# Deformable convolution block on one core: four instead of five pairs gathered ahead, and the first chunk's expansion among the last tap products

## What is computed

```python
# layer 0
out = relu(bn(conv1x1(x, w1)))                  # 1024 -> 256 channels
offset = conv3x3(out, w_off, b_off)             # 18 channels: (dy, dx) of 9 taps
out = relu(bn(deform_conv3x3(out, offset, w2))) # 4 bilinear corners of 9 taps per pixel
x1 = relu(bn(conv1x1(out, w3)) + x)             # 256 -> 1024 channels
# layer 1
t, p, g = Wt @ x1, Wp @ x1, Wg @ x1             # 1024 -> 512 each
att = sum over pixels and channels of (1, p, p**2) * g
y = polynomial of second order in t with att
z = Wz @ y                                      # 512 -> 1024
return groupnorm(z) * gn_w + gn_b + x1
```

## Time and profile before

| | us |
|---|---|
| median of 3 runs (2628.82 to 2649.33) | 2645.32 |
| the profiled execution | 2640.11 |
| its span, first to last instruction | 2638.3 |
| TensorE, VectorE, ScalarE, POOL busy | 2333.8, 1561.7, 1233.0, 687.2 |

### The profile page before, as it was taken

How to read it: one execution, slowest core, us unless ns; L and a number is a source line. 1 busy time by engine, 2 the same in 40 slices (tenths; PEclk the granted TensorE clock), 3 DMA queues, 4 the chain that set the end, 5 groups by cost and what they waited for, 6 DMA issues and landing times.

```text
span 2638.3 us, 29349 instructions
## 1 busy us (share of the span) xinstructions
PE 2333.8 (88%) x10316; PEld 1921.2 (73%) x10316; DVE 1561.7 (59%) x3126; ACT 1233.0 (47%) x2393; POOL 687.2 (26%) x613
## 2 busy tenths in 40 slices
PE   7999997998863699999999999999999999987730
PEld 5888886777753587888888888888888878866530
DVE  4113115446345788889888889988842244544464
ACT  5444343333222455656655565665532244444454
POOL 0000013323341344455554455555400000000000
PEclk9999998898886899999999999999999999998875
DMA  7999999999996698899899889998931111144469
GB/s 255 285 290 269 293 277 336 311 350 294 341 286 254 234 327 316 320 342 340 316 327 328 314 325 339 340 321 326 324 134 68 56 36 48 64 147 160 157 245 390
DMA packets 328012, 691.68 MB, mean 262 GB/s; under 512 B 20664, under 2 KB 170040, under 8 KB 321464
## 3 DMA queue, kind: packets, MB, share of 16 engines
q1 hardware_dynamic: 225464, 327.28, 39.1%
q0 software_dynamic: 83968, 303.80, 32.4%
q10 hardware_dynamic: 18432, 58.73, 5.6%
HBM read 443.38 MB, written 246.35 MB: 261 GB/s over the span
## 4 chain that ended last, share of the span: by engine, by line
PE 73%; DMA 14%; DVE 6%; ACT 3%; SPq 2%; issue 2%; POOL 0%; ACTq 0%; DVEq 0%
PE bank L136 20%; PE bank L138 20%; PE bank L137 20%; DMA vwide<-vb 7%; PE bank L1239 4%; PE bank L1240 4%; PE bank L1241 4%; DMA xt<-x 2%; DVE z L1183 1%; PE bank L1263 1%; DMA tb<-t 1%; DMA xin<-in_x 1%; DVE zst L1153 1%; SPq L360 1%; DMA stage<-in_wl 1%
## 5 line engine op out<-in xcount | busy, mean ns | idle before, releaser
L555 POOL DMA_INDIRECT g<-vwide,tbl x576 | 667.3, 1158 | 853.6 <-DVE a L864 402.3
L136 PE MATMUL bank<-x1h,wlh 128*128 128x512 f32 x1536 | 603.8, 393 | 2.9 <-DVE x1l L1070 2.9
L138 PE MATMUL bank<-x1h,wll 128*128 128x512 f32 x1536 | 600.9, 391 | 0.0
L137 PE MATMUL bank<-x1l,wlh 128*128 128x512 f32 x1536 | 600.3, 391 | 0.0
L880 DVE SCALAR_TENSOR_TENSOR a<-g,tbl,a 128x256 f32<-128x256 f32 x1258 | 538.3, 476 | 28.6 <-DMA g<-vwide,tbl 27.0
L574 ACT ACTIVATE g<-g,tbl 128x256 f32<-128x256 f32 x972 | 409.9, 499 | 185.2 <-DMA g<-vwide,tbl 168.9
L136 PEld LDWEIGHTS bank<-x1h,wlh 128*128 128x128 f32 x1536 | 289.3, 188 | 64.1 <-issue 3.3
L138 PEld LDWEIGHTS bank<-x1h,wll 128*128 128x128 f32 x1536 | 289.0, 188 | 62.2
L137 PEld LDWEIGHTS bank<-x1l,wlh 128*128 128x128 f32 x1536 | 289.4, 188 | 61.0
L1239 PE MATMUL bank<-w2h,o1h 128*128 128x512 f32 (+1 forms) x640 | 249.0, 389 | 68.3 <-ACT vb L627 68.3
L627 ACT ACTIVATE vb<-bank 128x512 f32<-128x512 f32 (+1 forms) x320 | 166.9, 556 | 293.8 <-DMA vwide<-vb 212.4
(11 more groups left out here) (141 smaller groups left out, 3108.3 us busy)
## 6 DMA issues: line engine op xcount, KB each, us to landing
vwide<-vb SPq DMA_DIRECT2D x128, 1152.0 KB
xin<-in_x SPq DMA_DIRECT2D x64, 512.0 KB
xf<-in_x SPq DMA_DIRECT2D x32, 1024.0 KB
x<-xf ACTq DMA_DIRECT2D x32, 1024.0 KB, 6.6
out<-z SPq DMA_DIRECT2D x128, 256.0 KB, 4.4
xb<-x SPq DMA_DIRECT2D x38, 512.0 KB, 4.0
t<-ts ACTq DMA_DIRECT2D x64, 256.0 KB
tb<-t SPq DMA_DIRECT2D x16, 1024.0 KB, 5.1
```

The source lines that it names most:

```text
L136: nc.tensor.matmul(out, wh, xh, start=first, stop=False)
L137: nc.tensor.matmul(out, wh, xl, start=False, stop=False)
L138: return nc.tensor.matmul(out, wl, xh, start=False, stop=last)
L555: pool.indirect_dma_start(slot[:].rearrange("p a c -> p (a c)"), None, d["vwide"][img], bass.IndirectOffsetOnAxis(ap=at[:, i, tap(u), 0:1] ...
```

## The change

1. `ALONE` is 4, and `f_points` puts 36 units (four pairs) in the front: from step 10 on at points 1, 2, 3 and 5 of each step. All other units move up in P, still 18 per chunk. `sums_due` stores a pair's sum one point behind its completion instead of two, from the end of the front on.
2. Chunk 0's transposes, `o2(0)`, expansion, residual and x1 stand in steps 16 and 17, with buffers of their own: `ACL0` (in stage buffer 2), `O2H0`, `O2L0`, and PSUM banks 0 and 1. `x1_high(0, k)` stays behind the front. Pairs 0 and 1 are loaded in step 15, `XF` before the last four tiles' stores, and weight blocks 2 to 6 between those stores.
3. First step: three more x blocks ahead of W2; W2 is loaded and split in five column groups, behind `o1(0)`; the stores of zero pads go from SP's queue to POOL's.

```diff
-ALONE = 5
+ALONE = 4
...
-            if s == 9 and point > 2 or 10 <= s <= 16 and point not in (0, 4) or s == 17 and point < 6:
+            if s == 9 and point > 2 or s > 9 and point in (1, 2, 3, 5):
...
-... if e + 2 == k]
+... if e + (2 if e < len(F_ENDS) - 2 else 1) == k]
...
+    ACL0 = m.put("acl0", [128, TILES, CMID], at=STAGE_AT[2])
+    O2H0, O2L0 = (m.put(n, [128, KMID, NPX], f32r, at=R5 + at * KB) for n, at in (("o2h0", 5), ("o2l0", 20)))
...
@@ SP, first step
-            for k in range(KMID):
-                sp.dma_start(W2R[:, k, :], d["w2"][:, k, :]).then_inc(w2_in[k], 16)
+            for i in range(XR, 2 * XR):
+                load_x(i)
+            for j, (lo, hi) in enumerate(VGROUPS):
+                if j == 2:
+                    load_x(2 * XR)
+                sp.dma_start(W2R[:, :, lo:hi], d["w2"][:, :, lo:hi]).then_inc(w2_in[j], 16)
...
@@ SP, steps
                 if s == ALLC - 1:
-                    for w in range(3):
+                    for p in range(2):
+                        sp.wait_ge(ao_out, 16 * (p + 1))
+                        sp.dma_start(ACL0[:, 2 * p:2 * p + 2, :], d["acc"][p]).then_inc(acl0_in[p], 16)
+                    for w in range(2):
                         stage(w)
                 if s == ALLC:
-                    stage(3)
+                    for h in range(2):
+                        load_xf(0, h)
                 if s:
                     for t in range(TILES):
                         store_v(s - 1, t)
...
-                        if s == ALLC and t < 3:
-                            stage(4 + t)
+                        if s == ALLC and t == 0:
+                            sp.wait_ge(tr_done, TILES)
+                            stage(2)
+                        if s == ALLC and t:
+                            stage(2 + t)
+                        if s == ALLC and t == 3:
+                            stage(6)
...
             def load_acl(p):
-                if p == 0:
+                if p == 2:
                     for b in range(2):
                         sp.wait_ge(vb_out[b], vb_count(TILES * ALLC, b))
                 sp.wait_ge(ao_out, 16 * (p + 1))
-                at_least(sp, tr_done, 2 * p)
+                sp.wait_ge(tr_done, 2 * p)
                 sp.dma_start(ACL[:], d["acc"][p]).then_inc(acl_in, 16)
-            for h in range(2):
-                load_xf(0, h)
-            load_acl(0)
-            for w in range(7, 9):
-                stage(w)
-            load_acl(1)
-            for w in range(9, 12):
+            for w in range(7, 12):
                 stage(w)
...
@@ POOL: pads() moved here from SP
+            pool.wait_ge(o1_done, KMID * 3)
+            pads()
...
@@ ScalarE
                 if s == ALLC:
-                    for w in range(4):
+                    for w in range(2):
                         split_high(w)
...
                 if tiles:
                     v_evict(s - 1, 0)
+                if s == ALLC:
+                    o2(0)
+                if s == 0:
+                    w2_high(0)
+                    w2_high(1)
                 if 4 * s + XR + 3 < 4 * ALLC:
                     x_high(4 * s + XR + 3)
+                if s == 0:
+                    for j in range(2, len(VGROUPS)):
+                        w2_high(j)
...
+                if s == ALLC:
+                    for w in range(2, 4):
+                        split_high(w)
                 store_sums(7 * s + 3)
                 store_sums(7 * s + 4)
                 if tiles:
                     v_evict(s - 1, 2)
+                if s >= ALLC:
+                    x1_pair(0, 2 * (s - ALLC))
                 store_sums(7 * s + 5)
                 if tiles:
                     v_evict(s - 1, 3)
+                if s >= ALLC:
+                    x1_pair(0, 2 * (s - ALLC) + 1)
...
@@ VectorE: o2_low(0) behind f_gather(s, 1), residual_pair(0, ..) behind f_gather(s, 4) and (s, 6), s = 16 and 17
@@ TensorE
                 if 1 <= s <= ALLC:
                     taps(s - 1, 0)
+                if s == ALLC:
+                    for i in range(TILES):
+                        transposes(0, i)
+                if 1 <= s <= ALLC:
                     taps(s - 1, 1)
                 if s >= 2:
                     offsets(s - 2)
+                if s >= ALLC:
+                    expand_pair(0, 2 * (s - ALLC))
                 if 1 <= s <= ALLC:
                     taps(s - 1, 2)
                 if s >= 2:
                     select(s - 2)
+                if s >= ALLC:
+                    expand_pair(0, 2 * (s - ALLC) + 1)
                 if 1 <= s <= ALLC:
                     taps(s - 1, 3)
-            for i in range(TILES):
-                transposes(0, i)
-            for o in range(KIN):
-                expand(0, o)
```

More of the change, by code:

```diff
@@ L1043, in _ @@
                     nc.vector.tensor_copy(Y[2][:, :, 0:SIDE - 1], Y[1][:, :, 1:SIDE]).then_inc(ys_done, 1)
+                if s == ALLC:
+                    for w in range(2, 4):
+                        split_low(w)
                 f_gather(s, 4)
+                if s >= ALLC:
+                    residual_pair(0, 2 * (s - ALLC))
                 if s >= 2:
@@ L1105, in _ @@
             v.wait_ge(sums_set, IMGS)
-            o2_low(0)
-            for k in range(KIN):
-                residual(0, k)
             for k in range(KIN):
@@ L1227, in taps @@
                 tile, r = TILES * s + t, s % 3
-                if tile == 0:
-                    pe.wait_ge(w2l_done, KMID)
                 if t == 0:
@@ L1265, in select, with transposes, expand_pair @@
                 last.then_inc(op_done, 1)
+            def transposes(n, i):
+                if n == 0 and i == 0:
+                    pe.wait_ge(cst_in, 48)
+                    pe.wait_ge(o1_done, KMID * ALLC)
+                if n == 1 and i == 0:
+                    pe.wait_ge(off_done, ALLC)
+                if i == 0:
+                    at_least(pe, xr_done, KIN * n)
+                if i % 2 == 0 and n:
+                    pe.wait_ge(acl_in, 16 * (2 * n + i // 2 - 1))
+                elif i % 2 == 0:
+                    pe.wait_ge(acl0_in[i // 2], 16)
+                for k in range(KMID):
+                    tile = ACL[:, i % 2, 128 * k:128 * k + 128] if n else ACL0[:, i, 128 * k:128 * k + 128]
+                    last = nc.tensor.transpose(transpose_bank(n, k)[:, 128 * i:128 * i + 128], tile, IDENT[:])
+                last.then_inc(tr_done, 1)
+            def expand_pair(n, i):
+                high, low = o2_tiles(n)
+                if n == 0 and i == 0:
+                    pe.wait_ge(wl_done, 2)
+                if i == 0:
+                    pe.wait_ge(o2l_done, KMID * (n + 1))
+                if n == CHUNKS + 1 and i == 0:
+                    pe.wait_ge(coef_done, 1)
+                for o in (2 * i, 2 * i + 1):
+                    at_least(pe, xr_done, KIN * n + o - 3 if n else o - 1)
+                    for k in range(KMID):
+                        last = product(nc, expansion_bank(n, o)[:], W3H[:, k, 128 * o:128 * o + 128], W3L[:, k, 128 * o:128 * o + 128],
+                                       high[:, k, :], low[:, k, :], k == 0, k == KMID - 1)
+                    last.then_inc(w3_done, 1)
             for s in range(ALLC + 2):
```

219 lines of the change are left out of this document (108 added, 111 removed).

## The result

| | before | after |
|---|---|---|
| median of 4 runs, us | 2644.07 (2628.82 to 2649.33) | 2673.07 (2671.01 to 2678.99) |
| the profiled execution | 2640.11 | 2678.99 |
| its span | 2638.3 | 2677.0 |
| P's first project matmul, in the trace | 852.6 | 814.8 |
| Z begins | 2112.6 | 2150.7 |

The ratio of the times is 1.0131, with an interval of 1.0103 to 1.016. The kernel became slower by 1.3%; the forecast was 2666, +21 us, and the medians differ by 29. The two traces differ by 38.7: the profiled execution of the changed kernel is the slowest of its four, 6 us above the median, and that of the kernel before lies 4 us under its own.

The account below looks back on a forecast made before the run. P (twelve projections for each of 16 chunks) was taken as bound by TensorE, the late front by DMA. The front's -54 us and P's +75 gave +21: 2645 + 21 = 2666 us, range 2596 to 2712.

Parts of the forecast that it names:

- P: thirteen waits and the clock: In P, chunks 1 to 13 each lose 5.8 us to a TensorE stall and slower clock: +75 us.
- the front: Before P: fewer gathers, earlier first step, interleaved end; P starts at 798.4 instead of 852.57, -54 us, bounds -40 and -72.
- The wait: In P behind group 2, TensorE's transposes wait 4.2 us for the sums' store and load, 5.84 us each.
- Rival 1: In P, store and load together stay under 7.5 us, so only the front's gain is left: 2591; chance 0.15.
- rival 2: In P, stalls of 5 to 6 us and 3 us of half clock in 13 chunks: 2712; chance 0.17.
- The clock: In P, TensorE's matmuls run at half clock behind each stall: 1.6 us more per stall, bounds 0 and 3.2.
- One point instead of two gains nothing: In P, storing the sums one point behind the fold gains nothing: ScalarE already issued at 1048.16.
- There DMA is the bound: Late front's steps with gathers: DMA sets their time, 2.5 us per unit; nine units less give -22 us, bounds 21 and 27.
- What must still come last is the sixth weight block (w = 5): End of the front: this block, issued behind the last store and split before x1_high, adds 3 us before P.
- First step, -4: Start of the front: TensorE's first wait goes, the second shrinks by half; -4 us, bounds 0 and -10.
- The first chunk of P keeps its 105.10: P's first chunk stays at 105.10 us, its stalls hanging on weight blocks, table(3) and loads in the old order.
- The moved wait of 14.79 us: Late front: a weight-block wait that stopped TensorE for 14.79 us changes place and keeps its size.

Follow-up runs that it names:

- 0.987: The changed kernel with transposes (n, 2) and (n, 3) one group later in each chunk of P, behind group 3: ratio 0.987 to the kernel before.
- control: The kernel before, unchanged, run once more for a trace from the same chip as the experiments: 2623.35 us.

## Why the prediction was right

| term | predicted | by the pair of traces | by the timed runs |
|---|---|---|---|
| P: thirteen waits and the clock | +75 | +75.9 | +69 (1.0131 - 0.987) |
| the front | -54 | -37.8 | -34 (0.987) |
| sum | +21 | +38.7 | +29 (medians), +35 (ratio) |

The forecast of 2666 had the change at +0.8%, inside the 1% that the prediction called no difference (0.42); the measured 1.3% lies among the slower ones, to which it gave 0.36. The sum came within 8 us by the medians and within 18 by the traces, and nearly all of what it missed is the front.

**The wait.** Right in its mechanism, its place, its count and its size. TensorE transposes pair 2c+3 in chunk c behind group 2; c = 0 and c = 14 are spared; the fold ends at +9.3 us of the chunk as before. Store and load were reckoned at 5.84 each, 11.68, and took 4.70 + 6.61 = 11.3; the wait at 4.2, and is 3.83; the clock behind it at 1.6, and costs 6.02 - 3.83 = 2.2. The errors are small and of opposite signs, so 5.8 per chunk came out as 6.02. The 75.9 us of P are twelve chunks at 6.02, 3.0 for c = 1 and 0.6 for the first chunk. The price was taken from the one row where the same tile was loaded beside P's gathers. That row decided rightly against the quiet one, but how near it came is in part luck: the changed kernel's loads in the first chunk took 5.5 to 14.8 us. From 900 us on, over 27 loads of sums, the load took at least 2.7 us, 6.6 in the middle and 7.3 at most, as the view of line 459 has it:
```profile
DMA to landing us min/median/max: 2.7/6.6/7.3
```
The 2.7 is the last of them, in c = 14, where no gather is left, and as long as the quiet one of the earlier trace rows; with 2.0 for the store before it, it fits in the 7.5 us, as the prediction said of c = 14. Rival 1 needed 3.75 for each, and fell by 3.8 us; rival 2 needed 5 to 6 us of wait.

The Trainium skill (DMA: Bandwidth & Descriptors, Anatomy of one DMA) gives a fit, for DMAs that POOL issues; by it, as an estimate, this load from SP's queue takes 2.6 us. The trace agrees for the quiet load and disagrees for the median one by 4.0 us. The same page of the Trainium skill (Latency and other measured facts) puts the HBM access latency at 0.2 us on average and 2 us at high load, and says that the fixed cost shrinks with a lighter load; that has the direction of what is seen here at a DMA share of 0.86, but no run here separates latency from queueing behind the gathers.

**The clock.** The forecast charged each wait its own loss of clock, and this is what the stretches show: 0.96 to 0.98 granted in the three chunks shown alone, 0.97 over the next ten together, 1.00 in a chunk with no wait. The rule that a wait repeated in every tile pays for the clock in every tile (the Trainium skill, TensorE: Matmul & The Clock Gate, HAM oscillation) agrees with the trace: 2.2 us for each of the twelve waits of c = 2 to 13, 26 us in all.

**One point instead of two gains nothing.** Right: 49.8 and 49.0 us of waits with and without it.

**The front: right in its sign, too large by 16 to 20 us.** It can be split at the two traces' marks. The first store of step 8 comes 11.2 us earlier (368.8 against 380.0); from there to the end of the five steps nothing is gained (319.8 us against 318.4); the last part gains 28.0. TensorE's stretches in the two traces behind the five steps, those of the kernel before first:
```profile
698.40:754.40 56.00, 36.18 (x157) 30.45 (x156) 20.19 (x45) 14.62 (x26) 18.46 (x10) 0.79 0.91 299
754.40:852.60 98.20, 50.48 (x218) 41.19 (x217) 47.31 (x109) 20.60 (x34) 33.61 (x23) 0.72 0.79 273
```
```profile
688.60:729.80 41.20, 32.67 (x164) 27.23 (x163) 16.74 (x40) 12.84 (x23) 16.11 (x11) 0.92 1.05 327
729.80:784.40 54.60, 37.48 (x154) 31.10 (x154) 22.73 (x50) 13.92 (x25) 10.88 (x8) 0.78 0.89 284
```
The last 30.40 us of the changed kernel's front, 784.40 to 814.80, stand in the table of the first section. 154.2 us have become 126.2, with a last stretch in which TensorE is busy for a third. This last part, from the first store of chunk 14's tap products to P's start, varies little between executions, and the other traces split it:

| end of the front | units ahead | traces | us |
|---|---|---|---|
| as before | 45 | 3 | 150.2 to 154.2 |
| as before | 36 | 1 | 140.3 |
| interleaved | 45 | 1 | 134.5 |
| interleaved | 36 | 6 | 123.2 to 126.2 |
| interleaved | 35 | 2 | 112.5 and 113.1 |

So the interleaved end is worth 14 to 20 us here, and the nine units 8 to 14, though only four of the nine stood in these last steps. (With seven units in each of steps 16 and 17, as in the run with three in a step, the interleaved end takes 134.2.) P's start itself is 802.1 to 814.8 in the six traces of the fourth row and 852.6 and 836.2 in the two of the kernel before, means that lie 36 apart: none of the six reached 798. Three of the prediction's steps are mis-sized or fail here.

1. *"There DMA is the bound", 2.5 us per unit, -22.* The price per unit fails, and the term is too large. Steps with three, four and five units take the same time within the scatter of the traces, with a DMA share of 0.93 and of 1.01. The nine units are worth 15 us in timed runs between two kernels without the wait, and 12 on the kernel before, and by the table most of that is gained in the last steps. A step of the late front is 41.0 us of a full TensorE and some 11 us of idle time and lost clock behind ScalarE's waits for stores. In the changed kernel those waits are still there (waits from 380 to 784 us, as the earlier trace rows):
```profile
ACT vb L648 <- DMA vwide<-vb: 112.5, 12, 15.2
...
PE bank L1298 <- ACT vb L648: 65.0, 11, 12.3
```
ScalarE's are down from 157.1 to 112.5, over a stretch that ends 36 us sooner, and TensorE's have stayed, 65.0 for 65.6. What sets the length of these waits is open. The number of units does not; six gathers in the first 11 to 20 us of each of the five steps stand in every trace, and were never taken away or spread.

2. *"What must still come last is the sixth weight block (w = 5)."* Wrong: last comes VectorE's residual and x1_low behind the front's last unit. The prediction counted the units of steps 16 and 17, four in each, as traffic, not as instructions that wait for a gather ahead of the moved residuals on VectorE. Taking the last of them out shortened the end of the front by 10 to 14 us, by the table's last two rows. Without any unit less, the interleaved end is worth 19 us in timed runs together with the first step, where the prediction had 28 + 4 for these; of the waits of TensorE that it removed (before: 20.7 on the sums' loads, 14.5 on the selection) more than half came back as one of 19.8 us at P's start. The changed kernel's waits of TensorE from 688.6 to 820 us:
```profile
PE bank L136 <- DVE x1l L1133: 19.8, 1, 19.8
```

3. *First step, -4.* Up to the first store of step 8 the traces named here are 5 to 11 us ahead with it, more than reckoned. Alone it is worth 0 in the timed runs, where anything from a gain of 5 us to a loss of 3 stays possible. The gain was summed into P's start as if the late front passed it on; it doesn't pass on all of it, and whether it passes on 4 us is not shown.

**The first chunk of P keeps its 105.10.** Right, 105.70. **The moved wait of 14.79 us.** It is 12.33 in the changed kernel, still a single long one in TensorE's timeline there:
```profile
767.00 0.58 PE L1298 MATMUL bank<-w2h,o1h 128*128 128x256 f32 x1 [12.33 <-ACT vb L648]
```

**The mark that was set.** "If P starts later than 815, the front's term fails": it starts at 814.8. The term is inside that mark by a hair and off by nearly a third, so the mark was set too wide to catch it.

## What to carry to other kernels

When work is put off to relieve one stage, follow every product of it to its consumer and write down the time left in the steady state: here 7.5 us for a store and a load through HBM, and one group of matmuls (5.5 us) decided between 1.3% slower and 1.3% faster. Price a transfer by the same transfer among the same neighbours, not by a quiet one (6.6 us against 2.7 for 256 KB), and add the clock's loss to each repeated wait of TensorE. A DMA share near 1 over a step does not price the traffic in it: vary the traffic before counting on its removal. And look in the trace whether an edit did what it was made for before reading its time: here six gathers came in 11.4 us with the edit that was to spread them, and in 11.8 without.

## What the hardware showed that was not expected

- The clock's price of a wait doesn't grow with it: 2.2 us behind waits of 3.83, 2.4 behind waits of 9.0.
- Removing two of five units from each late step lowered the DMA share from 1.02 to 0.93 and the traffic from 329 to 285 GB/s (control and three units) and left the five steps at 256 and 260 us.
- Two executions of one kernel differ by 16.4 us at P's start and by 1.3 us in P's length: the variation between executions sits in the front, where TensorE and ScalarE wait for DMA, and not in P, where TensorE is full.
- Of the same 256 KB in P, the load takes longer than the store: 6.6 against 5.0 us in the middle, over 27 of each in the changed kernel (store, line 601):
```profile
DMA to landing us min/median/max: 2.0/5.0/6.4
```
